# A macaron block on one core: norm of the third stage dealt over attention phases 1 and 2, maxima to their rows in two transfers

## The chip, the cores and the metric

The kernel runs on one core of one Trainium2 chip, as one program with one launch. The metric is the device time of the core in microseconds (us), the median of several executions.

## What is computed

A transformer block of three stages on x of shape (4, 256, 512), all in 32-bit floats: an FFN with half weight, attention, and the same FFN again. The FFN weights come as 4-bit numbers, W = scale[g] * (wq - (zq[g] + 1)), 512 to 2 x 1376 and back; attention has 32 heads of 16 columns with one shared key and value head, and is causal.

```python
x = x + 0.5 * ffn(layernorm(x))
x = x + attn(layernorm(x))
x = x + 0.5 * ffn(layernorm(x))
def ffn(x):
    inter = x @ w_gu
    gate, up = inter[..., :1376], inter[..., 1376:]
    return (silu(gate) * up) @ w_d
def attn(x):
    q, k, v = split(x @ Wqkv)
    scores = q @ k.T * 16 ** -0.5 + slope[h] * (pos_k - pos_q)
    return softmax(scores) @ v @ Wo
```

## The kernel before

The 1024 tokens are 8 tiles of 128. Every FFN stage runs in two halves of four tiles, numbered s = 0 to 3: s = 0 and 1 are the first FFN, s = 2 and 3 the third stage. Inside a half, 11 blocks j of the hidden width are taken in turn: gate and up matmuls (`gate_up`, L1395), silu on ACT (ScalarE), the product on DVE (VectorE), and `down` (L1421). Each product of full precision is three matmuls over a high and a low part of both operands. So an operand that comes out of PSUM is copied by ACT (the high part, `xt_high`, L643) and subtracted by DVE (the low part, `xt_low`, L892).

Attention goes sample by sample, in phases b = 0 to 3. Each phase has 12 units n; three units make a group o of 8 heads. In unit (b, n) TensorE computes `shifted_scores` (L1519, banks 4 and 5), ACT takes their exponentials (`exps`, L727), GpSimd masks them (L608), and TensorE multiplies by the values (`near_values` L1533 when n % 3 is 0, `far_values` L1544 when it is 1). ACT and DVE gather the sums (`even_heads` L737, `odd_heads` L1175, both when n % 3 is 2), TensorE swaps them (`swap_sums`, L1554), and DVE divides (`normalise`, L1188 and L1190). The output projection of a sample (`project_out`, L1561) runs one phase later, in the unit numbers that a list in TensorE's `between` gives, and DVE adds it to x (`attn_out`, L1196).

The softmax needs the row maximum first. In the phase before its own, a sample's plain scores are computed (`scores`, L1479 and L1487, banks 6 and 7, the units that `score_units` gives), and DVE reduces them (`maxima`, L1129) into `nm`. When all 12 are there, TensorE transposes `nm` (`max_transposes`, L1498), ACT copies the high part into `two` (`max_high`, L703), DVE makes the low part (`max_low`, L1136), and ACT issues four transfers (`max_to_rows`, L712) that put the 2 x 32 rows of `two` into four rows of `qp[b]`, the moving operand of the shifted scores. `shifted_scores(b, 0)` waits for them on the semaphore `m_in[b]`. Other transfers into `qp` (16 rows of constants, `constant_rows`, and the q rows, `q_to_rows`) are on the SP queue.

The third stage starts in the shadow of attention. Its first four tiles are those of samples 0 and 1. DVE takes `moments` (L843, L846), an inverse root by Newton steps (`rstd_seed`, `rstd_step`, from L852), and the normalised tile (`xn_tile`, L886), of which there are two buffers. TensorE transposes it (`ffn_transposes`, L1361). `xt` lies on the memory of `qp_c`, the operand of phase 2, so `xt_high(2, ...)` waits until the last shifted scores of phase 2 are done. Gate and up matmuls of half 2 fill TensorE in phase 3: `fill` does in unit n as many steps (three matmuls each) as the list in `fill_steps` says.

The order of the work on each engine is written out by hand: one loop over (b, n) on TensorE, ACT and DVE, each with a function `between` for all that isn't a unit's own work. Every engine runs its instructions in order. What sets the order around the change is where a call stands in these loops, and the tables of unit numbers.

```python
            for b in range(B):
                for n in range(NU):
...
                    between(b, n)
                    for unit in units[-1:]:
                        maxima(*unit)
```

## Time and profile before

| | us |
|---|---|
| median of 3 runs | 614.86 |
| lowest and highest | 614.31 and 631.7 |
| the profiled execution | 614.43 |
| its span, first to last instruction | 612.6 |

The profile shows one execution. Its times count from the start of the span. A row of a timeline gives start, length, engine, line, operation, output<-inputs, sizes, the count of merged instructions, and in square brackets how long the engine had been idle before and what released it. PEld is the weight load of TensorE (PE). ACTq and SPq are the issues of transfers on those engines' queues. In phase 0 to 3 the units of the profile are found by the tiles: `qp_a` is read in phases 0 and 3, `qp_b` in phase 1, `qp_c` in phase 2.

### The profile page before, as it was taken

What the parts mean: (1) busy time and instruction counts of PE and PEld (TensorE: products, weight loads), DVE (VectorE), ACT (ScalarE), POOL (GpSimd) and SP (SyncE); (2) the same over time, 40 slices, a digit from 0 to 9 for tenths busy, and PEclk for the clock granted to TensorE, in tenths of its full rate; (3) what the DMA queues carried; (4) which work ended last, traced back from release to release, by engine and by line L of the source; (5) the groups of instructions that cost most, each with busy time, mean ns of one, the idle gap of its engine ahead of it and who ended that gap; (6) DMA issues with size and microseconds to landing.
All of it is one profiled execution on the core that took longest, in us unless ns stands there. A gap on an engine that the chain in (4) does not pass through costs nothing.

```text
span 612.6 us, 7685 instructions
## 1 busy us (share of the span) xinstructions
PE 559.6 (91%) x2968; PEld 405.8 (66%) x2968; DVE 335.8 (55%) x705; ACT 160.7 (26%) x286; POOL 88.9 (15%) x113
## 2 busy tenths in 40 slices
PE   1399999999999999979799899699999999999997
PEld 1278777778788667656455344356678887888885
DVE  5888999866311355677467899855411245111112
ACT  1242332322111011134523444464111112111110
POOL 4678000000310000021211222131000000000000
PEclk9999999999999999989889999799999999999999
DMA  7489511099057291205843000000790000100001
GB/s 206 152 251 277 147 31 39 13 247 431 8 102 132 76 120 18 39 2 102 144 87 52 4 2 1 6 1 1 237 294 1 1 0 18 51 2 0 1 0 68
DMA packets 40267, 51.52 MB, mean 84 GB/s; under 512 B 10700, under 2 KB 28214, under 8 KB 39832
## 3 DMA queue, kind: packets, MB, share of 16 engines
q1 hardware_dynamic: 35392, 40.13, 26.5%
q0 software_dynamic: 2656, 10.57, 5.4%
q10 hardware_dynamic: 2184, 0.35, 0.4%
q8 instruction: 23, 0.38, 0.3%
q14 instruction: 12, 0.10, 0.0%
HBM read 35.82 MB, written 15.02 MB: 83 GB/s over the span
## 4 chain that ended last, share of the span: by engine, by line
PE 58%; DVE 9%; ACT 1%; DMA 1%; issue 1%; ACTq 0%; DVEq 0%
PE bank L1395 25%; PE bank L1421 12%; PE bank L1561 4%; PE bank L1487 3%; PE bank L1454 3%; DVE nm L1129 3%; PE bank L1479 3%; PE bank L1533 2%; PE bank L1519 2%; PE bank L1554 2%; DMA qp_b<-two 1%; PE bank L1435 1%; PE bank L1439 1%; DVE stats L843 1%; PE bank L1361 1%
## 5 line engine op out<-in xcount | busy, mean ns | idle before, releaser
L1421 PE MATMUL bank<-w_d,hs 128*128 128x512 f32 (+1 forms) x528 | 131.1, 396 | 3.3 <-DVE w_d L944 1.8
L1421 PEld LDWEIGHTS bank<-w_d,hs 128*128 128x128 f32 (+1 forms) x528 | 97.6, 188 | 27.9 <-issue 5.4
L953 DVE TENSOR_TENSOR hf<-sil,bank 128x512 f32<-128x512 f32 (+1 forms) x44 | 30.1, 684 | 151.9 <-PE bank L1395 151.7
L1395 PE MATMUL bank<-xt,w_far 128*128 128x512 f32 (+1 forms) x384 | 92.5, 394 | 0.0
L1395 PE MATMUL bank<-xt,w_mid 128*128 128x512 f32 x384 | 90.6, 391 | 0.0
L1395 PE MATMUL bank<-xt,w_near 128*128 128x512 f32 x288 | 73.3, 406 | 10.0 <-DVE w_near L922 9.4
L1395 PEld LDWEIGHTS bank<-xt,w_mid 128*128 128x128 f32 x384 | 72.0, 188 | 15.4 <-issue 0.5
L1395 PEld LDWEIGHTS bank<-xt,w_far 128*128 128x128 f32 (+1 forms) x384 | 69.3, 181 | 18.2
L1129 DVE TENSOR_REDUCE nm<-bank 128x2 f32<-128x512 f32 (+1 forms) x96 | 61.7, 685 | 31.5 <-PE bank L1487 31.0
L1395 PEld LDWEIGHTS bank<-xt,w_near 128*128 128x128 f32 x288 | 54.2, 193 | 24.5 <-issue 12.2
L674 ACT CAST hs<-hf 128x512 fp32r<-128x512 f32 (+1 forms) x44 | 27.3, 621 | 130.9 <-DVE hf L953 118.0
L664 ACT ACTIVATE sil<-bank 128x512 f32<-128x512 f32 (+1 forms) x44 | 26.3, 597 | 127.8 <-PE bank L1395 127.4
L959 DVE TENSOR_TENSOR hs<-hf,hs 128x512 fp32r<-128x512 f32 (+1 forms) x44 | 32.5, 739 | 19.4 <-ACT hs L674 19.3
L1361 PE MATMUL bank<-ident,xn 128*128 128x128 f32 x96 | 17.2, 327 | 22.3 <-DVE xn L886 21.8
L1188 DVE RECIPROCAL den<-bank 128x128 f32<-128x128 f32 x32 | 30.4, 949 | 9.6 <-PE bank L1554 9.6
L1454 PE MATMUL bank<-xa,wqkv 128*128 128x256 f32 x128 | 31.5, 397 | 0.0
L1361 PEld LDWEIGHTS bank<-ident,xn 128*128 128x128 f32 x96 | 13.1, 166 | 26.4 <-issue 21.1
L608 POOL TENSOR_SCALAR_AFFINE_SELECT pt_a<-pt_a 128x512 f32<-128x512 f32 x16 | 10.4, 648 | 135.9 <-ACT pt_a L727 135.9
L1479 PE MATMUL bank<-causal,ident_b 128*128 128x256 bf16 (+1 forms) x96 | 22.7, 319 | 7.1 <-DVE nm L1129 6.2
L1454 PEld LDWEIGHTS bank<-xa,wqkv 128*128 128x128 f32 x128 | 24.6, 197 | 6.1 <-issue 2.8
L727 ACT ACTIVATE pt_a<-bank 128x512 f32<-128x512 f32 x32 | 17.4, 596 | 37.2 <-PE bank L1519 37.2
L1561 PE MATMUL bank<-wo,at_t 128*128 128x512 f32 x48 | 25.0, 627 | 0.0
(148 smaller groups left out, 566.5 us busy)
## 6 DMA issues: line engine op xcount, KB each, us to landing
gate_up_part<-w_mid SPq DMA_DIRECT2D x1, 4096.0 KB, 15.5
q_rows<-qst SPq DMA_DIRECT2D x16, 256.0 KB, 4.8
w_mid<-gate_up_part SPq DMA_DIRECT2D x4, 1024.0 KB, 8.3
gate_up_part<-w_far SPq DMA_DIRECT2D x1, 3840.0 KB, 24.0
qp_a<-q_rows SPq DMA_DIRECT2D x24, 128.0 KB, 4.4
w_far<-gate_up_part SPq DMA_DIRECT2D x3, 1024.0 KB, 9.0
raw_d<-in_L_ffn_qweight_down SPq DMA_DIRECT2D x10, 256.0 KB, 3.5
x<-in_L_attn_hidden_states SPq DMA_DIRECT2D x8, 256.0 KB, 5.0
```

What stands on the lines that cost most here:

```text
L664: nc.scalar.activation(sil[0:jw(jt(s, p)), n % 2, :], gate_bank(s, p)[0:jw(jt(s, p)), :], ACT.Silu)\
L674: nc.scalar.copy(hs[0:jw(jt(s, p)), n % 2, 0, :], hf[0:jw(jt(s, p)), n % 2, :]).then_inc(h_hi, 1)
L953: nc.vector.tensor_tensor(hf[0:jw(jt(s, p)), n % 2, :], sil[0:jw(jt(s, p)), n % 2, :], up_bank(s, p)[0:jw(jt(s, p)), :], ALU.mult).then_in ...
L959: nc.vector.tensor_tensor(hs[0:jw(jt(s, p)), n % 2, 1, :], hf[0:jw(jt(s, p)), n % 2, :], hs[0:jw(jt(s, p)), n % 2, 0, :].bitcast(F32), ALU ...
L1129: nc.vector.tensor_reduce(nm[:, min(u, 1), 2 * h0 + s:2 * (h0 + heads) + s - 1:2], bank[6 + s][:, :].rearrange("p (h n) -> p h n", h=heads ...
L1188: st.did(nc.vector.reciprocal(den[:, cols], ps))
L1361: ins = nc.tensor.transpose(ps[:, k * P:(k + 1) * P], xn[:, n % 2, k * P:(k + 1) * P], ident[:, :])
L1395: ins = nc.tensor.matmul(ps[0:jw(j), :], w_gu(a, k, gu, j), xt[:, b, k, :], start=(k == 0 and q == 0), stop=(k == KT - 1 and q == 2))
L1421: ins = nc.tensor.matmul(acc(s, t)[:, :], hs[0:jw(j), n % 2, a, t * P:(t + 1) * P], w_d[0:jw(j), j, b, :], start=(p == 0 and q == 0), stop ...
L1454: ins = nc.tensor.matmul(q_bank(b, h)[:, m * S:(m + 1) * S], wqkv[:, k, (2 * h + m) * P:(2 * h + m + 1) * P], xa[:, k, :], start=(k == 0), ...
L1479: nc.tensor.matmul(ps[:, :, 4 * P // heads - P:], ident_b[:, :], causal[:, :].unsqueeze(1).to_broadcast([P, heads, P]), start=True, stop=F ...
L1561: ins = nc.tensor.matmul(out_bank(b, t)[:, :], normed(b)[:, k, t * P:(t + 1) * P], wo[:, k, :], start=(k == 0), stop=(k == KT - 1))
```

## The change

Five parts:

- The maxima of a sample go to their rows in two transfers of 32 rows instead of four of 16; for that `nm` keeps the heads of each half side by side. `m_in` counts to 32 instead of 64.
- For samples 2 and 3 the transposes of the maxima stand right behind `near_values` of unit 9, ACT's `max_high` ahead of the exponentials of unit 9, and the transfers for sample 2 one unit sooner. Those for sample 3 are issued on SP (`last_max_to_rows`).
- On DVE a new function `after(b, n)` runs behind a unit's maxima. Into it go `attn_out` of sample 1 (units 5 and 8 instead of 6 and 9) and the norm of the third stage: moments tile by tile in (1, 9), (2, 1), (2, 7), (2, 9), and the first two tiles' root and normalised tiles at (2, 6) and (2, 10). The projection steps of sample 1 move to match.
- The last two of the four tiles are normalised by ACT (`act_xn`), with a shift `nmr` = -mean * rstd that DVE makes.
- TensorE transposes tile 0 in (2, 10) and tile 1 in (2, 11), tiles 2 and 3 in (3, 0) as before. `fill_steps` takes its step out of unit 1 and puts one more into unit 7.

```diff
@@ -303,7 +305,7 @@
 
-            count = (0, 1, 2, 0, 2, 2, 0, 1, 2, 0, 2, 2, 2)
+            count = (0, 0, 2, 0, 2, 2, 0, 2, 2, 0, 2, 2, 2)
             return range(sum(count[:n]), sum(count[:n + 1]))
@@ -452,6 +454,15 @@
 
+            def last_max_to_rows(b):
+
+                sp.wait_ge(a_mhi, b + 1)
+                sp.wait_ge(a_mlo, b + 1)
+                sp.wait_ge(q_in[b], 16 * 14)
+                for r in range(2):
+                    sp.dma_start(qp[b][18 + r:83 + r:64, :, :].bitcast(F32), two[0:NH, r, :].bitcast(F32))\
+                        .then_inc(m_in[b], 16)
+
             constant_rows(0)
@@ -472,6 +483,7 @@
                 q_to_rows(3, h)
+            last_max_to_rows(B - 1)
             sp.wait_ge(a_st, 2 * NU * B)
@@ -642,6 +654,16 @@
 
+            def act_xn(s, t):
+
+                act.wait_ge(nmr_ok, 1)
+                act.wait_ge(tr_ok, tile_no("ffn", s, t) - 1)
+                tile = 4 * (s % 2) + t
+                dst = xn[:, t % 2, :].rearrange("p (k e r) -> p k e r", k=KT, e=2)
+                src = x[:, tile, :].rearrange("p (r k e) -> p k e r", k=KT, e=2)
+                nc.scalar.activation(dst, src, ACT.Identity, bias=nmr[:, t - 2:t - 1],
+                                     scale=rstd[:, tile:tile + 1]).then_inc(xn_ok, 1)
+
             def gu_high(j):
@@ -684,7 +706,7 @@
                 if b >= 2:
-                    act.wait_ge(m_in[b - 2], 64)
+                    act.wait_ge(m_in[b - 2], 32)
                 nc.scalar.copy(two[:, 0, :], kv_bank(b)[:, 0:S]).then_inc(a_khi, 1)
@@ -707,10 +729,9 @@
                 act.wait_ge(q_in[b], 16 * 14)
-                for s in range(2):
-                    for r in range(2):
-                        act.dma_start(qp[b][64 * s + 18 + r:64 * s + 19 + r, :, :].bitcast(F32),
-                                      two[s:NH:2, r, :].bitcast(F32)).then_inc(m_in[b], 16)
+                for r in range(2):
+                    act.dma_start(qp[b][18 + r:83 + r:64, :, :].bitcast(F32), two[0:NH, r, :].bitcast(F32))\
+                        .then_inc(m_in[b], 16)
@@ -799,14 +820,18 @@
                     k_high(b + 2)
-                if n == (8 if b == 0 else 9) and b + 1 < B:
-                    max_high(b + 1)
-                if n == (9 if b == 0 else 10) and b + 1 < B:
+                if (b, n) == (0, 8):
+                    max_high(1)
+                if (b, n) in ((0, 9), (1, 9)):
                     max_to_rows(b + 1)
-                if (b, n) in ((B - 2, NU - 1), (B - 1, 0)):
+                if (b, n) == (B - 2, NU - 1):
                     act.wait_ge(a_st, 2 * NU * (B - 1))
                     for t in range(2):
-                        xt_high(2, 2 * (b - B + 2) + t)
+                        xt_high(2, t)
+                        act_xn(2, t + 2)
+                if (b, n) == (B - 1, 0):
+                    for t in range(2, 4):
+                        xt_high(2, t)
@@ -815,6 +840,8 @@
                         even_heads(g)
+                    if n == 9 and 1 <= b < B - 1:
+                        max_high(b + 1)
                     exps(b, n)
@@ -1126,7 +1153,7 @@
                     dve.wait_ge(a_s, 2 * e + s + 1)
-                    nc.vector.tensor_reduce(nm[:, min(u, 1), 2 * h0 + s:2 * (h0 + heads) + s - 1:2],
+                    nc.vector.tensor_reduce(nm[:, min(u, 1), NS * s + h0:NS * s + h0 + heads],
                                             bank[6 + s][:, :].rearrange("p (h n) -> p h n", h=heads),
@@ -1273,34 +1300,42 @@
                         xn_tile(tile_no("attn", 3, 1), 7)
-                if (b, n) in ((1, 8), (1, 11), (2, 6), (2, 9)):
-                    attn_out(b - 1, int(n in (9, 11)))
-                if b == B - 2:
-                    if n == 1:
-                        dve.wait_ge(a_x, 2)
-                        moments(range(0, 2))
-                    if n == 2:
-                        rstd_seed(0, 0, 2)
-                    if n in (4, 5, 7):
-                        rstd_step(0, 0, 2)
-                    if n == 9:
-                        dve.wait_ge(a_x, 4)
-                        moments(range(2, 4))
-                    if n == 10:
-                        rstd_seed(0, 2, 4)
-                        for _ in range(3):
-                            rstd_step(0, 2, 4)
-                        st.wait()
-                        ffn_xn(2, 0)
-                        ffn_xn(2, 1)
-                    if n == 11:
-                        ffn_xn(2, 2)
-                        ffn_xn(2, 3)
+                if (b, n) in ((1, 8), (1, 11)):
+                    attn_out(0, int(n == 11))
                 if (b, n) in ((B - 2, NU - 1), (B - 1, 0)):
...
                     max_low(b + 1)
+
+            def after(b, n):
+
+                if (b, n) in ((2, 5), (2, 8)):
+                    attn_out(1, int(n == 8))
+                if (b, n) in ((1, 9), (2, 1), (2, 7), (2, 9)):
+                    tile = {(1, 9): 0, (2, 1): 1, (2, 7): 2, (2, 9): 3}[b, n]
+                    dve.wait_ge(a_x, tile + 1)
+                    moments(range(tile, tile + 1))
+                if b == B - 2:
+                    if n == 1:
+                        rstd_seed(0, 0, 2)
+                    if n in (2, 4):
+                        rstd_step(0, 0, 2)
+                    if n == 4:
+                        rstd_step(0, 0, 2)
+                    if n == 6:
+                        st.wait()
+                        ffn_xn(2, 0)
+                    if n == 9:
+                        rstd_seed(0, 2, 4)
+                    if n == 10:
+                        ffn_xn(2, 1)
+                        for _ in range(3):
+                            rstd_step(0, 2, 4)
+                        st.wait()
+                        nc.vector.scalar_tensor_tensor(out=nmr[:, :], in0=mv[:, 2:4, 0], scalar=-1.0,
+                                                       in1=rstd[:, 2:4], op0=ALU.mult, op1=ALU.mult)\
+                            .then_inc(nmr_ok, 1)
@@ -1317,6 +1352,7 @@
                         normalise(g - 2, 1)
+                    after(b, n)
             normalise(NO * B - 2, 0)
@@ -1504,7 +1540,7 @@
                 if n == 0:
-                    pe.wait_ge(m_in[b], 64)
+                    pe.wait_ge(m_in[b], 32)
                 if e >= 1:
@@ -1583,7 +1619,7 @@
                 if b in (1, 2):
-                    for q, step in enumerate(range(4, 12) if b == 1 else (1, 2, 4, 5, 6, 7, 8, 8)):
+                    for q, step in enumerate(range(4, 12) if b == 1 else (1, 2, 2, 4, 4, 5, 6, 7)):
                         if step == n:
@@ -1592,13 +1628,15 @@
                             project_out(b - 1, t, range(k, k + 1))
-                if (b, n) in ((B - 2, NU - 1), (B - 1, 0)):
-                    for t in range(2):
-                        ffn_transposes(2, 2 * (b - B + 2) + t)
+                if (b, n) in ((B - 2, NU - 2), (B - 2, NU - 1)):
+                    ffn_transposes(2, n - NU + 2)
+                if (b, n) == (B - 1, 0):
+                    for t in range(2, 4):
+                        ffn_transposes(2, t)
                 if b == B - 1:
                     fill(n)
-                if n == (8 if b == 0 else 9) and b + 1 < B:
-                    max_transposes(b + 1)
+                if (b, n) == (0, 8):
+                    max_transposes(1)
@@ -1680,6 +1718,8 @@
                             near_values(g - 1)
+                        if n == 9 and 1 <= b < B - 1:
+                            max_transposes(b + 1)
                     if n % 3 == 1 and g >= 1:
```

The first place is TensorE in unit 9 of phase 1. `bank_7<-ident,nm` is the transpose of the maxima, `bank<-wo,at_t` the output projection, `bank<-qp_b,kp` the shifted scores of a unit. Before:

```order
L1554 MATMUL bank<-den,swap 128x256
L1533 MATMUL bank<-pt_a,vp 32x256 x8
L1561 MATMUL bank<-wo,at_t 128x512
L1498 MATMUL bank_7<-ident,nm 32x128 x2
L1519 MATMUL bank<-qp_b,kp 128x512 x2
```

And in the changed kernel:

```order
L1590 MATMUL bank<-den,swap 128x256
L1569 MATMUL bank<-pt_a,vp 32x256 x8
L1534 MATMUL bank_7<-ident,nm 32x128 x2
L1597 MATMUL bank<-wo,at_t 128x512
L1555 MATMUL bank<-qp_b,kp 128x512 x2
```

The transposes moved ahead of one step of the projection; on ACT the copy that reads them moved from behind the two exponentials of that unit to ahead of them.

The second place is TensorE from unit 10 of phase 2 to unit 1 or 2 of phase 3. `bank<-qp_c,kp` are the shifted scores of phase 2, `bank<-qp_a,kp` those of phase 3, `bank<-ident,xn` the transposes of normalised tiles (four to a tile). Before:

```order
L1519 MATMUL bank<-qp_c,kp 128x512 x2
L1544 MATMUL bank<-pt_far,vp 32x128 x8
L1519 MATMUL bank<-qp_c,kp 128x512 x2
L1361 MATMUL bank<-ident,xn 128x128 x8
L1519 MATMUL bank<-qp_a,kp 128x512 x2
L1554 MATMUL bank<-den,swap 128x256
L1533 MATMUL bank<-pt_b,vp 32x256 x8
L1361 MATMUL bank<-ident,xn 128x128 x8
L1519 MATMUL bank<-qp_a,kp 128x512 x2
L1544 MATMUL bank<-pt_far,vp 32x128 x8
L1395 MATMUL bank_7<-xt,w_near 128x512 x3
```

And in the changed kernel:

```order
L1555 MATMUL bank<-qp_c,kp 128x512 x2
L1580 MATMUL bank<-pt_far,vp 32x128 x8
L1397 MATMUL bank<-ident,xn 128x128 x4
L1555 MATMUL bank<-qp_c,kp 128x512 x2
L1397 MATMUL bank<-ident,xn 128x128 x4
L1555 MATMUL bank<-qp_a,kp 128x512 x2
L1590 MATMUL bank<-den,swap 128x256
L1569 MATMUL bank<-pt_b,vp 32x256 x8
L1397 MATMUL bank<-ident,xn 128x128 x8
L1555 MATMUL bank<-qp_a,kp 128x512 x2
L1580 MATMUL bank<-pt_far,vp 32x128 x8
L1555 MATMUL bank<-qp_a,kp 128x512 x2
```

The transposes of tile 0 moved one unit up, and the first three gate matmuls are gone from unit 1 of phase 3.

The third place is DVE at the same handover, from the last Newton step of the inverse root on. `num` and `den` are the odd heads of unit 11, `xt` the low parts. Before:

```order
L869 SCALAR_TENSOR_TENSOR rstd<-nwt,rstd 128x2
L886 TENSOR_SCALAR xn<-x,mv,rstd 128x512 x2
L1175 SCALAR_TENSOR_TENSOR num<-bank,pmask,num 128x256
L1175 SCALAR_TENSOR_TENSOR den<-bank,pmask,den 128x256
L886 TENSOR_SCALAR xn<-x,mv,rstd 128x512 x2
L892 TENSOR_TENSOR xt<-bank,xt 128x4x128 x2
L1188 RECIPROCAL den<-bank 128x128
```

And in the changed kernel:

```order
L896 SCALAR_TENSOR_TENSOR rstd<-nwt,rstd 128x2
L1336 SCALAR_TENSOR_TENSOR nmr<-mv,rstd 128x2
L1202 SCALAR_TENSOR_TENSOR num<-bank,pmask,num 128x256
L1202 SCALAR_TENSOR_TENSOR den<-bank,pmask,den 128x256
L919 TENSOR_TENSOR xt<-bank,xt 128x4x128 x2
L1215 RECIPROCAL den<-bank 128x128
```

Four normalised tiles left this place: tile 0 went to unit 6, tile 1 ahead of the Newton steps, tiles 2 and 3 to ACT, and the shift came in.

## Rows read from the trace of the kernel before

**Rows 1.** The page's chain that ended last: its shares by engine.

```profile
PE 58%; DVE 9%; ACT 1%; DMA 1%; issue 1%; ACTq 0%; DVEq 0%
```

**Rows 2.** Chain in order of time, end of phase 0: start us, us, what.

```profile
294.96 0.48 ACTq L712
...
296.11 7.03 DMA qp_b<-two
```

**Rows 3.** Issues of the maxima's transfers: count, size, median us to landing. First 294.7:295.2, then 340:400.

```profile
qp_b<-two ACTq DMA_DIRECT2D x2, 16.0 KB, 6.3
...
qp_a<-two ACTq DMA_DIRECT2D x4, 16.0 KB, 2.2
```

**Rows 4.** Stretches: us, TensorE busy (count), granted clock (1 is full), DMA share, GB/s.

```profile
300.00:302.00 2.00, 0.00 (x0) 0.81 1.74 239
311.50:312.00 0.50, 0.50 (x3) 1.00 1.15 135
386.50:387.00 0.50, 0.00 (x0) 0.59 0.06 18
```

**Rows 5.** Timeline of TensorE, units 0 and 2 of phase 1.

```profile
303.18 0.80 PE L1519 MATMUL bank<-qp_b,kp 64*128 64x512 f32 x2 [4.41 <-DMA qp_b<-two]
...
308.94 3.24 PE L1454 MATMUL bank<-xa,wqkv 128*128 128x256 f32 x8
...
315.21 1.99 PE L1454 MATMUL bank<-xa,wqkv 128*128 128x256 f32 x8
```

**Rows 6.** Timelines of TensorE and ACT, units 9 and 10 of phase 1.

```profile
342.52 1.12 PE L1561 MATMUL bank<-wo,at_t 128*128 128x512 f32 x2
343.49 0.38 PE L1498 MATMUL bank<-ident,nm 128*32 128x128 f32 x2
343.80 0.50 PE L1519 MATMUL bank<-qp_b,kp 64*128 64x512 f32 x2
...
341.06 1.08 ACT L727 ACTIVATE pt_b<-bank 128x512 f32<-128x512 f32 x2 [0.68 <-PE bank L1519]
343.90 0.36 ACT L703 CAST two<-bank 32x256 fp32r<-32x256 f32 x1 [1.76 <-PE bank L1498]
```

**Rows 7.** Timeline of TensorE, end of phase 2 and phase 3.

```profile
388.00 1.09 PE L1361 MATMUL bank<-ident,xn 128*128 128x128 f32 x4 [5.10 <-DVE xn L886]
...
390.38 0.79 PE L1519 MATMUL bank<-qp_a,kp 64*128 64x512 f32 x2
391.10 1.22 PE L1554 MATMUL bank<-den,swap 128*128 128x256 f32 x2
...
394.82 0.50 PE L1519 MATMUL bank<-qp_a,kp 64*128 64x512 f32 x2
...
399.60 0.51 PE L1519 MATMUL bank<-qp_a,kp 64*128 64x512 f32 x2
...
409.33 0.96 PE L1395 MATMUL bank<-xt,w_near 128*128 128x512 f32 x3
```

**Rows 8.** Timelines of DVE and, one row, of POOL (GpSimd), end of phase 2.

```profile
378.58 1.29 DVE L1129 TENSOR_REDUCE nm<-bank 128x2 f32<-128x512 f32 x2 [0.45 <-PE bank L1487]
...
380.98 0.68 DVE L1196 TENSOR_TENSOR x<-x,bank 128x512 f32<-128x512 f32 x1
...
383.18 0.38 DVE L1136 TENSOR_TENSOR two<-bank,two 32x256 fp32r<-32x256 f32 x1
...
384.66 0.16 DVE L852 TENSOR_SCALAR nwt<-mv 128x2 f32<-128x2 f32 x1
...
387.11 2.17 DVE L886 TENSOR_SCALAR xn<-x,mv,rstd 128x512 f32<-128x512 f32 x2
389.20 0.47 DVE L1175 SCALAR_TENSOR_TENSOR num<-bank,pmask,num 128x256 f32<-128x256 f32 x1
...
389.99 1.39 DVE L886 TENSOR_SCALAR xn<-x,mv,rstd 128x512 f32<-128x512 f32 x2
...
387.52 1.29 POOL L608 TENSOR_SCALAR_AFFINE_SELECT pt_far<-pt_far 128x1024 f32<-128x1024 f32 x1 [4.48 <-ACT pt_far L727]
```

2 lines of the change are left out of this document (added).

## The prediction

> **What bounds the kernel now.** I read the chain that ended last first. The reader is to see that most of it is TensorE [rows 1]: 58% of the chain, with DVE (VectorE) at 9%. The first and the last stage are matmuls back to back, and an edit there would show at full price. The change touches the attention stage between them, so I read that stage stall by stage in the timelines of TensorE, DVE and ACT (ScalarE). I write (b, n) for unit n of phase b, as the code does. Two long stalls stand there.
>
> The first is at the start of phase 1. ACT issues four transfers that bring the maxima of sample 1 to their rows; the fourth is issued at 296.11 and takes 7.03 us [rows 2], and TensorE waits 4.41 us for it, until 303.18 [rows 5]. The same transfers take 2.2 us in a phase where nothing else is in flight [rows 3]. The difference is the company: the SP queue moves the q rows of sample 2 and then the constant rows of sample 3 at that time.
>
> The second is at the end of phase 2. TensorE waits 5.10 us, until 388.00, for the first normalised tile of stage 3 [rows 7]. DVE makes it in a row [rows 8]: x update at 380.98, then moments of two tiles, the low part of the maxima at 383.18, half a normalise, the inverse root from 384.66, two tiles at 387.11, and only at 389.20 the odd heads. Phase 3 then opens at 390.38, and its second unit stands at 394.82 [rows 7].
>
> Each stall also takes TensorE's clock from 2.4 to 1.2 GHz. It fell between 300 and 302, TensorE being idle since 298.8 (303.18 less 4.41), and was back at 311.5; in the other stall it fell between 386.5 and 387.0, idle since 382.9 [rows 4, 7]. What that costs is seen in one group of eight matmuls: 3.24 us at the low level, 1.99 at the high one [rows 5].
>
> **The change part by part.**
>
> **A, two transfers for four.** Before the start of phase 1 the order of the work stays; only the transfers become two of 32 rows each. The chain shows the second issue at 294.96 and the fourth 1.15 later [rows 2]. The median of the first two is 6.3 us to landing and the fourth took 7.03 [rows 2, 3], so I put the second at 6.6: it landed at about 301.5, the fourth at 303.14. If a transfer twice as large lands like the small one, phase 1 starts 1.7 us sooner. The lower end of the gain is 0 (the bytes are the same, and they land with the last of the four); the upper end is the whole stall, 4.4 (with the 2.2 us of the quiet phase they would be there at 297.2). I take 1.7, the row of the very transfer. The clock falls all the same, since it fell within 300 to 302 and TensorE now idles until 301.5. If it comes back sooner, up to 1.2 us more is won in the eight matmuls at 308.94 (3.24 less 1.99); the sum takes nothing of it. For sample 0, in the first FFN stage, TensorE shows no wait for these transfers: 0.
>
> A rule of the Trainium skill makes A smaller ("DMA: Bandwidth & Descriptors", section "Issuing engines are not separate DMA queues"): all queues run on the same 16 engines, and how a transfer is issued saves only the sequencer's time. The trace agrees on the sharing (7.03 us against 2.2). By the rule two saved issues count, 1.15 us, and the sum would be 0.55 less of a gain.
>
> **B, maxima sooner in phase 1.** In unit (1, 9) the transposes of the maxima move ahead of one output projection (342.52 to 343.49), and ACT's copy moves ahead of the unit's two exponentials [rows 6]. The exponentials now wait behind transposes that stand behind the values' matmuls. The transposes start at 342.52, the copy 0.41 later (343.90 less 343.49) and takes 0.36; 0.1 later two exponentials, 1.08 together [rows 6], run to 344.5. TensorE's shifted scores of (1, 10), which wait for them, stood at 343.80 and now stand at about 344.55: a loss of 0.75. The other end is 0.3, were the projection to cover more of it. The gain is nothing, since no wait for sample 2's transfers shows at the start of phase 2. DVE's moments of tile 0 go behind the second half of that unit's normalise, where DVE then waits for scores anyway: 0.
>
> **C, phase 2 and the opening of phase 3.** DVE works nearly without a gap in phase 2, so what is put ahead of the last maximum of sample 3 (378.58, done 379.87 [rows 8]) delays it. Ahead of it stand as before the moments of two tiles, one x update and one inverse root; new is one normalised tile, 0.69 (half of 1.39; half of 2.17 for a pair beside a GpSimd select [rows 8]). Besides, the two Newton steps in (2, 4) and the x update in (2, 5) now stand ahead of odd heads for which TensorE's swap matmul waits. Together 0.7 to 2.5; I take 1.8 by laying these pieces behind one another, so the maximum ends at 381.7. From there, with lengths from rows 8: x update 0.7, half a normalise 1.2, low maxima 0.3, the other half 1.2, moments of one tile 0.75, inverse root 2.45 (384.66 to 387.11), one tile 0.7, the shift 0.2, odd heads 0.8 (389.20 to 389.99). That is 8.3 us, so the odd heads end at about 390.0, as before; but before, two more tiles stood behind them. TensorE meanwhile: transposes of the maxima at 382.1, ACT's copy to 382.9, exponentials to 384.1, units 10 and 11 and the first two tiles' transposes until 388.1, and the first unit of phase 3 at 388.1 (before: 390.38). Then it waits for the odd heads until 390.1. Before, the swap stood at 391.10: 1.0 us is won there. At the high clock swap, values and the last two transposes take 3.0 us, and the second unit stands at 393.1 for 394.82: 1.7 won. ACT's two tiles (0.6 each by the length of an exponential, 1.1 at most as on DVE) end by 391.5, before TensorE wants the second. Before, the fourth unit (399.60) waited for the even heads behind DVE's two low copies and a normalise; these come 1.9 sooner, and the gate step of unit 1 is out of the way. That step comes back in unit 7, 0.96 [rows 7], of which 0.7 is not hidden. So C is -1.9 + 0.7 = -1.2 at the high clock. If the clock falls in the three gaps (382.5 to 384.1, 386.2 to 387.5, 388.6 to 390.1), 1.3 of it is lost and C is +0.1. None of these gaps is over 1.6 us, and both stalls that took the clock were of 4.4 and 5.1, so I take -1.2. The maxima's transfers, issued at 384.0 on SP, land by 387.0, and phase 3 wants them at 388.1; on SP only waits for the end of attention are queued behind them.
>
> The Trainium skill speaks against one piece of C ("SBUF — State Buffer", section "Who interferes with whom"): a VectorE operation of this kind and a GpSimd operation exclude each other, and the second waits for the whole of the first. The trace agrees: the pair at 387.11, beside the select at 387.52, took 2.17 us, the next pair 1.39 [rows 8]. By it the tile in (2, 10) costs 0.4 more, and the sum would be 0.4 less of a gain.
>
> **The sum.** -1.7 + 0.75 - 1.2 = -2.15 us against the profiled execution's 614.43 (span 612.6 and 1.8 around it): 612.3. The median of the runs shown, 614.86, is 0.4 higher, so I forecast 612.7. The new layout of the maxima (a reduce writes them side by side instead of in every second place) I cost at 0: the reduce's length is set by the 512 columns that it reads.
>
> **The rivals.**
> First, the transfers land when SP's traffic lets them, not sooner for being two. For it: each next one took longer, up to 7.03 us. Then A is 0 to -0.3, and the time 614.86 - 0.2 + 0.75 - 1.2 = 614.2. Against it: the later ones were issued into the constant rows' traffic, which two issues forestall.
> Second, the clock does better: it is back before or within the matmuls from 303 to 311.5. At half clock at most 4.1 of these 8.3 us are lost; 2.8 of them won back gives 609.9. Against it: the stall is still 2.7 us long.
> Third, slower than before: DVE's queue in phase 2 becomes the bound of the handover. Place: the odd heads of (2, 11), now behind the inverse root, a tile and the shift. Price: the maximum 2.5 late instead of 1.8, the tile beside a select 0.4, the clock fallen across the opening of phase 3 1.3, and still low for units 1 to 3 with their gate step (4 us of matmuls at twice the time, half of it hidden) 2.0: 4.4 on 612.7 is 617.1. It decides from C = +0.95 on, that is when the odd heads end after about 391 with the clock low.
> Fourth, the change does not do what it says, for nothing waited for the maxima of samples 2 and 3, so that sooner brings nothing: this is so by the trace and is in the forecast already.
>
> **How the numbers follow.** Forecast 0.50 (611.5 to 613.9), first rival 0.17, second 0.20, third 0.13. The range reaches to 609.5 for the second and to 616.5 for the third, which leaves its far end out. A measurement of this kernel can tell about 2%, 12 us, from no change, and no case comes near: faster 0.01, within 0.98, slower 0.01.
>
> **What would show it.** Right: phase 1 starts near 301.5; a new stall of 0.7 us before unit (1, 10); the 5.10 us stall gone, and in its place three of 1 to 2 us (before unit (2, 10), before the transposes of (2, 11), before the first swap of phase 3). Wrong: the second transfer for sample 1 takes 8 us; the last maximum of phase 2 is not later than before (then DVE was no bound there); the clock is at 1.2 GHz while phase 3 opens; an ACT table load stands beside the new tiles.

## The result and the profile after

| | before | changed |
|---|---|---|
| median, us | 623.04 (4 runs) | 623.21 (4 runs) |
| lowest and highest | 614.31 and 631.7 | 620.6 and 624.42 |
| the profiled execution | 614.43 | 624.42 |
| its span | 612.6 | 622.7 |

The ratio of comparable runs is 1.0135, 95% interval 1.0071 to 1.0199. (Two executions of before, at 631 us, are disturbed and not in the ratio; they are why the two medians look equal.) Forecast were 612.7 us, 0.35% less than before, and a range up to 616.5. The change makes the kernel slower.

The chain that ended last has the shares of before [rows 1], with one point more for DMA:

```profile
PE 58%; DVE 9%; DMA 2%; ACT 1%; issue 1%; SPq 0%; DVEq 0%; ACTq 0%
```

For the rest I measure stages by one kind of mark: the start of each unit's shifted scores in TensorE's timeline (every length below is the difference of two such starts; where no clock or transfer comes in they repeat within 0.02 us from run to run). Over the attention stage, in us:

| from, to | before | changed | difference |
|---|---|---|---|
| (0, 0) to (0, 11) | 38.52 | 43.15 | +4.63 |
| (0, 11) to (1, 0) | 4.91 | 5.16 | +0.25 |
| (1, 0) to (1, 9) | 37.40 | 37.65 | +0.25 |
| (1, 9) to (1, 10) | 3.22 | 3.78 | +0.56 |
| (1, 10) to (2, 0) | 8.17 | 8.16 | 0 |
| (2, 0) to (2, 9) | 26.41 | 30.91 | +4.50 |
| (2, 9) to (3, 0) | 12.00 | 9.24 | -2.76 |
| (3, 0) to (3, 3) | 9.22 | 12.20 | +2.98 |
| (3, 3) to (3, 11) | 17.30 | 17.98 | +0.68 |

The sum, +11.1, is the difference of the spans (10.1) and the 1.1 us by which (0, 0) started sooner. The rows answer to steps A (second and third), B (fourth) and C (the last four, +5.4). The first row is +4.2 in unit (0, 2) and +0.5 in (0, 3), and nothing elsewhere. TensorE, ACT and DVE have the same instructions there; only the columns of `nm` that DVE writes are others. I take it as not the change's, and the first two experiments bear on that.

TensorE's timeline of the changed kernel, the marks and the waits:

```profile
306.99 0.80 PE L1555 MATMUL bank<-qp_b,kp 64*128 64x512 f32 x2 [4.66 <-DMA qp_b<-two]
```

```profile
348.42 0.50 PE L1555 MATMUL bank<-qp_b,kp 64*128 64x512 f32 x2 [0.56 <-ACT pt_b L748]
...
366.63 0.70 PE L1590 MATMUL bank<-den,swap 128*128 128x256 f32 x2 [1.31 <-DVE den L1202]
...
376.88 1.22 PE L1590 MATMUL bank<-den,swap 128*128 128x256 f32 x2 [1.57 <-DVE den L1202]
...
386.68 0.39 PE L1515 MATMUL bank<-causal,ident_b 128*128 128x256 bf16 x2 [1.64 <-DVE nm L1156]
...
392.76 0.50 PE L1555 MATMUL bank<-qp_c,kp 64*128 64x512 f32 x2 [1.42 <-ACT pt_b L748]
...
396.14 0.66 PE L1397 MATMUL bank<-ident,xn 128*128 128x128 f32 x4 [1.15 <-DVE xn L913]
...
399.56 1.22 PE L1590 MATMUL bank<-den,swap 128*128 128x256 f32 x2 [2.33 <-DVE den L1202]
...
404.38 0.50 PE L1555 MATMUL bank<-qp_a,kp 64*128 64x512 f32 x2
```

Row by row: the wait for the maxima of sample 1 is as long as before (4.66 for 4.41 [rows 5]). A new wait of 0.56 stands before unit (1, 10). The swap matmul waits 1.31 and 1.57 us for `den`, in units (2, 3) and (2, 6): before, it waited for nothing there, as the row of unit (2, 6) below shows. The 5.10 us wait [rows 7] is gone, and 1.64, 1.42, 1.15 and 2.33 have come for it. The second unit of phase 3 stands 7.65 us behind the first, for 4.44 before [rows 7].

```profile
369.39 0.70 PE L1554 MATMUL bank<-den,swap 128*128 128x256 f32 x2
```

DVE (VectorE) in the same units, `nwt` and `rstd` being the inverse root, `num` and `den` the odd heads:

```profile
364.47 0.85 DVE L879 TENSOR_SCALAR nwt<-mv 128x2 f32<-128x2 f32 x1
...
365.70 0.48 DVE L1202 SCALAR_TENSOR_TENSOR num<-bank,pmask,num 128x256 f32<-128x256 f32 x1
...
374.50 0.95 DVE L896 SCALAR_TENSOR_TENSOR rstd<-nwt,rstd 128x2 f32<-128x2 f32 x1
...
375.96 0.48 DVE L1202 SCALAR_TENSOR_TENSOR num<-bank,pmask,num 128x256 f32<-128x256 f32 x1
```

```profile
382.27 1.29 DVE L1156 TENSOR_REDUCE nm<-bank 128x4 f32<-128x512 f32 x2 [2.46 <-PE bank L1523]
...
388.11 1.28 DVE L1156 TENSOR_REDUCE nm<-bank 128x2 f32<-128x512 f32 x2
...
396.39 0.96 DVE L896 SCALAR_TENSOR_TENSOR rstd<-nwt,rstd 128x2 f32<-128x2 f32 x1
...
398.63 0.48 DVE L1202 SCALAR_TENSOR_TENSOR num<-bank,pmask,num 128x256 f32<-128x256 f32 x1
399.03 0.48 DVE L1202 SCALAR_TENSOR_TENSOR den<-bank,pmask,den 128x256 f32<-128x256 f32 x1
```

And GpSimd's selects (POOL), of which two stand here:

```profile
374.36 1.09 POOL L620 TENSOR_SCALAR_AFFINE_SELECT pt_far<-pt_far 128x1024 f32<-128x1024 f32 x1 [2.73 <-ACT pt_far L748]
...
396.24 1.09 POOL L620 TENSOR_SCALAR_AFFINE_SELECT pt_far<-pt_far 128x1024 f32<-128x1024 f32 x1 [1.09 <-ACT pt_far L748]
```

Two things are to be seen. The odd heads come right behind pieces of the inverse root (the seed before 365.70, two steps before 375.96), and TensorE waits for them. And an operation on two elements a partition, 0.16 us alone, takes 0.95 when it meets a select: the one at 374.50 ends at 375.45, and the select that began at 374.36 ends at 375.45 too; the one at 396.39 ends at 397.35, the select at 397.33.

The granted clock, in stretches of the timeline (columns as in rows 4):

```profile
272.00:276.00 4.00, 4.00 (x26) 0.50 0.00 2
...
305.50:315.00 9.50, 7.75 (x35) 0.50 0.54 116
366.60:376.50 9.90, 8.59 (x68) 1.00 0.00 0
377.00:380.50 3.50, 3.50 (x19) 0.53 0.02 5
...
387.50:390.50 3.00, 2.87 (x18) 0.50 0.00 0
...
398.00:404.00 6.00, 4.44 (x25) 0.50 0.01 3
```

Five stretches at 1.2 GHz, 37.5 us together (264.3 to 277.9, 305.2 to 315.5, 376.9 to 380.3, 387.1 to 390.6, 397.4 to 404.2); before had three, 20.5 us together (263.7 to 267.1, 301.3 to 311.5, 386.6 to 393.4). The first two lie behind the same waits in both. That it stayed low for 13.7 us instead of 3.4 in phase 0 goes with the +4.6 of the table: 10.2 us more at half the clock are at most 5.1 us.

### The profile page after: what moved, and what is told of

Same layout as the page of the kernel before. It is cut to its first block, busy times and chain, and to the rows that moved or that the text cites. A ratio compares the mean times of both kernels' runs of the same rounds, so it can differ in the third digit from the quotient of the medians.

```text
span 622.7 us, 7679 instructions
## 1 busy us (share of the span) xinstructions
PE 567.5 (91%) x2968; PEld 410.3 (66%) x2968; DVE 336.2 (54%) x704; ACT 162.8 (26%) x288; POOL 89.2 (14%) x113
## 4 chain that ended last, share of the span: by engine, by line
PE 58%; DVE 9%; DMA 2%; ACT 1%; issue 1%; SPq 0%; DVEq 0%; ACTq 0%
PE bank L1431 25%; PE bank L1457 11%; PE bank L1597 3%; PE bank L1523 3%; PE bank L1569 3%; PE bank L1490 3%; DVE nm L1156 3%; PE bank L1515 2%; PE bank L1590 2%; DMA qp_c<-q_rows 2%; PE bank L1555 1%; PE bank L1471 1%; PE bank L1475 1%; PE bank L1580 1%; DVE xn L913 1%
```

## The experiments

Two theories stood at first. G: the added waits take the clock, so the loss stays whatever is done about the maxima. L: the loss is luck, the clock behind a wait that the change doesn't touch. All ratios are to before on the same chip, by comparable runs, with the 95% interval.

**e1, the changed kernel again.** No edit.

> The changed kernel as it is, timed against the kernel before in 5 rounds, to see how far each of them varies from run to run. Theory G (the gaps: the change puts work on DVE ahead of odd heads and of maxima, TensorE gets gaps of 1.3 to 2.3 us in phase 2 and at the opening of phase 3, and its clock falls in them): the profile again shows three falls of the clock between 370 and 405 us, and TensorE waits before the swaps; time 620 to 625. Theory L (luck: the time lost is the clock that happened to stay low after the stall at 262 us, which the change doesn't touch): this run varies as the kernel before does (614 to 632), and in a run where the clock comes back by 268 us the changed kernel is at 616 to 621.

Measured: 618.16 us, 1.0066 [1.0042, 1.0091]. In its profiled execution:

```profile
266.00:272.00 6.00, 5.78 (x21) 0.50 0.00 0
272.50:280.00 7.50, 6.74 (x58) 1.00 0.00 1
```

So both hold in part. The median lies below G's 620, but its three falls of the clock are there, and both waits for `den`. The clock in phase 0 came back at 272.5, not 277.9, and (0, 0) to (0, 11) took 40.56 us instead of 43.15: that share of the first result was luck. The rows of B and C repeat: (1, 9) to (1, 10) 3.77, (2, 0) to (2, 9) 30.80, (2, 0) to (3, 11) 70.48 for 70.33. Those of A do not: (0, 11) to (1, 0) is 4.25 for 5.16, (1, 0) to (1, 9) 36.77 for 37.65. What the change itself costs is 0.7%, 4 us.

**e2, two transfers alone.** The kernel before, with

```diff
-                for s in range(2):
-                    for r in range(2):
...
+                for r in range(2):
+                    act.dma_start(qp[b][18 + r:83 + r:64, :, :].bitcast(F32), two[0:NH, r, :].bitcast(F32))\
+                        .then_inc(m_in[b], 16)
```

and the layout of `nm` and the counts of `m_in` that go with it.

> The kernel before with nothing but two transfers of 32 rows instead of four of 16, for all samples. If transfers are bound by their issue (my step A) phase 1 starts 1.7 us sooner and the time is 1 to 3 us less. If the traffic of SP's queue binds them (the first rival) the stall at the end of phase 0 stays within 0.3 us of 4.41 and the time is the kernel's before, within 0.5 us, each state of the clock taken for itself.

Measured: 614.22 us, 1.0008 [0.998, 1.0037]. Nothing is gained. Its chain has the second transfer at

```profile
295.22 8.68 DMA qp_b<-two
```

that is, 0.55 us behind ACT's first issue, where the fourth of before stood 1.83 behind it (294.28 and 296.11): 1.3 us sooner, and 1.65 longer (7.03 [rows 2]). The interval leaves at most 1.2 us of gain, less than the 1.7 of step A.

**e3, the changed kernel with the maxima at their old place.** Phases 1 and 2:

```diff
-                if (b, n) == (0, 8):
-                    max_high(1)
...
+                if n == (8 if b == 0 else 9) and b + 1 < B:
+                    max_high(b + 1)
...
-                    if n == 9 and 1 <= b < B - 1:
-                        max_high(b + 1)
                     exps(b, n)
```

the same for `max_transposes`, and the transfers of sample 2 issued in unit 10.

> The changed kernel with the transposes and the high part of the maxima back in their old places (behind the exponentials of unit 9), transfers for sample 2 back in unit 10. Step B says that the gap of 0.56 us before unit (1, 10) and that of 1.42 us before unit (2, 10) go: 0.6 to 0.8 us less from phase 1, and up to 1 us less from phase 2, where DVE is late anyway. Theory G: it stays slower than the kernel before by 3 us or more, since the gaps on DVE's account stay. Theory L: no difference beyond the luck of the clock.

Measured: 618.5 us, 1.0067 [1.0039, 1.0095], that of e1. (1, 9) to (1, 10) is back at 3.22, but (2, 0) to (3, 11) is 70.52. The loss is not in the maxima. Its chain and TensorE's timeline hold one surprise:

```profile
296.35 5.52 DMA qp_b<-two
```

```profile
301.92 0.50 PE L1553 MATMUL bank<-qp_b,kp 64*128 64x512 f32 x2 [1.62 <-DMA qp_b<-two]
```

With the same two transfers the second took 5.52 us here, 7.63 in e1, 8.68 in e2, and (0, 11) to (1, 0) is 2.13 us for 4.91 before: this one time phase 1 did start sooner. Its company was the same (SP's six issues of q rows begin 2.1 us ahead of ACT's first issue here, 2.0 in e1, 1.9 in e2), so why it landed sooner is open. And though TensorE waited only 1.62 us, the clock was at 1.2 GHz from 302.6 to 309.4.

**e4, the maxima sooner alone.** The kernel before with the edit that e3 undoes, four transfers on ACT kept.

> The kernel before with only the transposes and the high part of the maxima ahead of the exponentials of unit 9 in phases 1 and 2, and the transfers for sample 2 one unit sooner; four transfers. Step B says 0.6 to 0.8 us slower in phase 1 (unit 10 waits for the exponentials). In phase 2 TensorE's unit 10 waits as well, 1 to 1.5 us, which the wait of 5.10 us for the first normalised tile swallows. Time 0.5 to 1 us above the kernel before in the same state of the clock.

Measured: 616.14 us, 1.0028 [1.0004, 1.0052]. (1, 9) to (1, 10) is 3.77, as in the changed kernel: this is B's price. The next unit takes 3.34 for 2.99, but that belongs to this run alone: with two transfers it is 2.98 in the changed kernel and 2.99 in e1. Sample 3's earlier maxima bring nothing back: (2, 0) to (3, 11) is 65.86, where e2 has 65.95.

So the loss of C should lie in where the norm stands. By units, (2, 3) to (2, 4) lost 1.4 us, its wait of 1.31, and (2, 6) to (2, 7) 3.2, its wait of 1.57 and 1.6 more with the clock low; both stand right behind the pieces put ahead of odd heads. The other units up to (2, 7) differ by projection steps that were moved, and even out within 0.2 us.

**e5, the norm behind the odd heads.** The changed kernel, with

```diff
-                if (b, n) in ((1, 9), (2, 1), (2, 7), (2, 9)):
-                    tile = {(1, 9): 0, (2, 1): 1, (2, 7): 2, (2, 9): 3}[b, n]
+                if (b, n) in ((1, 9), (2, 2), (2, 7), (2, 9)):
+                    tile = {(1, 9): 0, (2, 2): 1, (2, 7): 2, (2, 9): 3}[b, n]
...
-                    if n == 1:
+                    if n == 2:
                         rstd_seed(0, 0, 2)
-                    if n in (2, 4):
+                    if n in (3, 5):
                         rstd_step(0, 0, 2)
-                    if n == 4:
+                    if n == 5:
                         rstd_step(0, 0, 2)
```

> The changed kernel, with the norm work that stood ahead of odd heads in phase 2 put behind them: moments of tile 1 and the seed from unit 1 to 2, one Newton step from unit 2 to 3, two from unit 4 to 5. Same work, same count of instructions. Theory P (place): phase 2 lost 4.4 us between (2, 0) and (2, 9) because these pieces delay odd heads, TensorE's swap waits 1.31 and 1.57 us for them, and the second wait takes the clock. Then (2, 0) to (2, 9) falls from 30.9 us to 27 to 28.5, both waits for den go or fall under 0.5, and the kernel is 2 to 4 us faster than the changed one. Rival W (work): DVE is full in phase 2 and it is the added normalised tile and what it has to do, not its place, that sets the end; then (2, 0) to (2, 9) stays over 30 and the time within 1 us of the changed kernel.

Measured: 615.73 us, 1.0032 [1.0001, 1.0062]. (2, 0) to (2, 9) is 26.96 for 30.91, within 0.6 of before: theory P. TensorE's and DVE's timelines:

```profile
368.76 0.70 PE L1590 MATMUL bank<-den,swap 128*128 128x256 f32 x2
...
377.20 0.39 PE L1515 MATMUL bank<-causal,ident_b 128*128 128x256 bf16 x2 [1.85 <-DVE nm L1156]
...
389.97 0.70 PE L1590 MATMUL bank<-den,swap 128*128 128x256 f32 x2 [2.32 <-DVE den L1202]
```

```profile
378.64 1.27 DVE L1156 TENSOR_REDUCE nm<-bank 128x2 f32<-128x512 f32 x2
```

The swap at 368.76, which waited 1.57 us, waits for nothing, and (2, 3) to (2, 4) takes 2.99 us as before. The last maximum of phase 2 starts 27.5 us behind (2, 0); in the changed kernel it was 31.5, before 26.6. So the norm's work delays it by 0.9 us, and its place did by four more. The clock, which fell right behind the 1.57 us wait in the changed kernel, in e1 and in e3, stayed at 2.4 GHz until 377.5. Left is the opening of phase 3, with its wait of 2.32.

**e6, ACT's tiles alone.** The kernel before, where tiles 2 and 3 leave DVE:

```diff
                         ffn_xn(2, 0)
                         ffn_xn(2, 1)
-                    if n == 11:
-                        ffn_xn(2, 2)
-                        ffn_xn(2, 3)
+                        nc.vector.scalar_tensor_tensor(out=nmr[:, :], ...)
```

and `act_xn(2, t + 2)` behind `xt_high(2, t)` on ACT, as in the change.

> The kernel before with one part of the change alone: tiles 2 and 3 are normalised by ACT from a shift that DVE makes behind tiles 0 and 1; nothing else moves. If ACT's tiles are what opens phase 3 badly (they took 1.33 us each in the changed kernel, ahead of the exponentials of unit (3, 0)), (3, 0) to (3, 3) grows from 9.2 us by 1 to 2 here and the kernel is 0.5 to 1.5 us slower than before. If the bad opening comes from the order on DVE (inverse root and tile 1 ahead of the odd heads), (3, 0) to (3, 3) stays within 0.7 of 9.2 here and the time within 0.5 us of before, or up to 1 less, since DVE is rid of 1.39 us.

Measured: 616.36 us, 1.0023 [0.9987, 1.0058]: too close to call. (3, 0) to (3, 3) is 10.10, but with before's order there it is anything from 9.2 to 10.2 in the profiles of e2, e4, e7 and e8 as well. ACT's timeline, though, is plain:

```profile
387.49 1.33 ACT L654 ACTIVATE xn<-x,nmr,rstd 128x512 f32<-128x512 f32 x1
...
389.19 1.33 ACT L654 ACTIVATE xn<-x,nmr,rstd 128x512 f32<-128x512 f32 x1
390.41 1.08 ACT L739 ACTIVATE pt_a<-bank 128x512 f32<-128x512 f32 x2
```

A tile costs ACT 1.33 us, twice my 0.6, and the exponentials of (3, 0) stand behind both.

**e7, the q rows held.** The kernel before. SP waits before the second half of sample 2's q rows, and so before the constant rows behind them (the loop over the halves is written out for that):

```diff
-            for h in range(2):
-                q_to_dram(2, h)
-                q_to_rows(2, h)
+            q_to_dram(2, 0)
+            q_to_rows(2, 0)
+            q_to_dram(2, 1)
+            sp.wait_ge(m_in[1], 64)
+            q_to_rows(2, 1)
```

> The kernel before, but SP issues the second half of sample 2's q rows (six transfers of 128 KB), and the constant rows behind them, only when the maxima of sample 1 have landed. Theory S (the maxima land with SP's traffic, whatever their number): the fourth transfer takes 2 to 3.5 us instead of 7.03, TensorE's wait before unit (1, 0) falls from 4.4 to under 1 us; the scores of sample 2, which need the held rows, then wait 3 to 6 us in unit (1, 0), so the kernel is within 2 us of before, on either side. Rival F (a fixed cost of these 16-row writes): the fourth still takes over 5 us with nothing beside it, and the kernel is 4 us or more slower.

Measured: 616.85 us, 1.0046 [1.0014, 1.0078]. Its chain, and TensorE's timeline:

```profile
295.09 2.88 DMA qp_b<-two
...
300.22 5.96 DMA qp_c<-q_rows
```

```profile
299.07 0.50 PE L1521 MATMUL bank<-qp_b,kp 64*128 64x512 f32 x2 [1.32 <-ACT pt_far L729]
306.23 1.04 PE L1481 MATMUL bank<-causal,ident_b 128*128 128x512 bf16 x2 [6.66 <-DMA qp_c<-q_rows]
```

The fourth transfer takes 2.88 us, like the quiet 2.2 of [rows 3]: theory S. What is left of the wait, 1.32, is for exponentials. (0, 11) to (1, 0) is 1.82 us for 4.91, so A could hardly have won more than 3.1 us, and the transfers' number was not what it hung on. The held rows are then late themselves (6.66), and the kernel as a whole is slower.

**e8, a projection in the wait.** The kernel before. The eight matmuls that cost 3.24 us behind the wait [rows 5] go ahead of it:

```diff
-                if (b, n) in ((0, 8), (0, 10), (1, 0), (1, 2)):
+                if (b, n) in ((0, 8), (0, 10), (1, 2)):
...
+                    if (b, n) == (1, 0):
+                        project_q(3, 1, range(4))
                     shifted_scores(b, n)
```

> The kernel before, with the eight matmuls halves of the q projection of sample 3 that stand in unit (1, 0) put ahead of its shifted scores, into the wait for the maxima. If the wait's price is TensorE's idle time and the clock that it takes, the wait falls from 4.4 to about 2.4 us, the eight matmuls no longer cost 3.24 us behind it, and the kernel is 2 to 4 us faster than before. If the q work was hidden behind the maxima of sample 2 on DVE (4.29 us idle there, waiting for TensorE), the gain is under 1 us.

Measured: 609.92 us, 0.9934 [0.9894, 0.9973], faster than both kernels.

```profile
300.18 1.99 PE L1454 MATMUL bank<-xa,wqkv 128*128 128x256 f32 x8
304.66 0.50 PE L1519 MATMUL bank<-qp_b,kp 64*128 64x512 f32 x2 [2.49 <-DMA qp_b<-two]
```

The wait is 2.49 and (1, 0) to (1, 1) takes 6.55 us for 9.49, 2.9 less. By the ratio the kernel gained 4.1 us (1.7 to 6.5). The profiled execution is one of the slower of the eleven, at 613.78: four lie from 613.6 to 615.6 and seven from 607.0 to 611.0. What the seven have over it no profile shows.

**e9, odd heads first.** The kernel of e5, with the opening of phase 3 loosened. On DVE, in unit 11, and on ACT:

```diff
                         ffn_xn(2, 1)
-                        for _ in range(3):
-                            rstd_step(0, 2, 4)
+                        rstd_step(0, 2, 4)
...
+                if (b, n) == (B - 2, NU - 1):
+                    for _ in range(2):
+                        rstd_step(0, 2, 4)
...
-                        act_xn(2, t + 2)
+                if (b, n) == (B - 1, 0):
+                    act_xn(2, 2)
+                    act_xn(2, 3)
```

The shift stands behind the two steps; transposes and copies of tile 3 go to (3, 1).

> The kernel of e5 with the opening of phase 3 loosened: on DVE the odd heads of unit (2, 11) stand ahead of two of the three Newton steps and of the shift; on ACT the exponentials of (3, 0) stand ahead of its two tiles; the transposes and copies of tile 3 go to unit (3, 1). Theory O (the rest of C's loss is the odd heads behind the inverse root and the exponentials behind ACT's tiles): in e5 the swap of (3, 0) stood at 2.8 us behind that unit's scores, with TensorE waiting 2.32 us for den; that wait falls under 1 us and (3, 0) to (3, 3) falls from 11.5 us to 9 to 10, so the kernel is 1.5 to 2.5 us faster than e5, at a ratio of about 1.000 to before. Rival T (the tiles themselves are late): TensorE waits for ACT's tile 2 instead, by 1.5 us or more, and (3, 0) to (3, 3) stays over 11.

Measured: 614.43 us, 0.9992 [0.9962, 1.0022]. (3, 0) to (3, 3) is 10.28, (2, 0) to (3, 11) 64.19: below before's 64.93 for the first time in a kernel with the change's order. TensorE, and its clock:

```profile
388.41 0.70 PE L1594 MATMUL bank<-den,swap 128*128 128x256 f32 x2 [0.95 <-DVE den L1203]
...
391.48 0.63 PE L1401 MATMUL bank<-ident,xn 128*128 128x128 f32 x4 [1.37 <-ACT xn L664]
```

```profile
377.50:380.50 3.00, 3.00 (x17) 0.50 0.00 0
382.00:395.00 13.00, 7.68 (x76) 1.00 0.02 6
```

The wait for `den` fell from 2.32 to 0.95 (theory O), one of 1.37 for ACT's tile came (a part of T), and the clock does not fall there in this execution. That is not sure to be the order's doing: in e11, with the same opening, it fell at 387.3 and (3, 0) to (3, 3) took 11.08 us.

**e10, the whole projection.** As e8 with all sixteen matmuls: `project_q(3, 1)`.

> As e8, with all sixteen matmuls of the q projection of sample 3's second half ahead of the first shifted scores of phase 1 (from units 0 and 2). In e8 the wait left over was 2.49 us and the clock still fell. If idle time is what takes the clock, the wait is now about 0.5 us, the clock stays at 2.4 GHz from (1, 0) on, and (1, 0) to (1, 1), 6.55 us in e8, falls to 5 or less: 2 to 4 us faster than e8, 6 to 9 faster than before. If the clock falls all the same, or the q rows of sample 2 bind next, it is within 1.5 us of e8.

Measured: 612.6 us, 0.9974 [0.9944, 1.0003]: a miss. The profiled execution, 608.92, did what was foreseen:

```profile
297.36 3.72 PE L1454 MATMUL bank<-xa,wqkv 128*128 128x256 f32 x16
301.54 0.50 PE L1519 MATMUL bank<-qp_b,kp 64*128 64x512 f32 x2 [0.47 <-DMA qp_b<-two]
...
309.40 0.60 PE L1479 MATMUL bank<-causal,ident_b 128*128 128x512 bf16 x2 [1.33 <-DVE nm L1129]
```

A wait of 0.47, the clock up, (1, 0) to (1, 1) 3.86 us. But with unit 2 emptied, TensorE waits 1.33 for a maximum of sample 2, and there the clock fell (310.1 to 313.5). Over (1, 0) to (1, 9) it is 32.96 against 34.51 in e8, and still the ratio is 0.004 behind e8's, though the two intervals overlap. Why most executions gained less than the profiled one is open.

**e11, all mends together**: the changed kernel with the edits of e5, e9 and e8, and sample 2's maxima at their old place. **e12, e8 again** beside it.

> The changed kernel with all mends: norm behind odd heads (e5), opening of phase 3 as in e9, the eight matmuls in the wait (e8), and sample 2's maxima back behind the exponentials of (1, 9). If the parts add up: e9 stood at 0.999 of before, e8 at 0.993, and unit (1, 10) gives 0.56 us back, so 0.991 to 0.993, about 609.5 us where before is 614.6; (1, 9) to (1, 10) is 3.2 again, (2, 0) to (3, 11) 64.2. If the clock's answer to a removed stall eats the gain, as it may have in e10, 0.996 or more.

> The kernel of e8 again, beside e11 on one chip. It stood at 609.92 us, 0.9934, its profiled execution at 613.78 with TensorE's clock low from 264.2 to 271.5 and again to 312.0. If the spread of 607 to 615 is how long the clock stays low behind the waits, a profiled execution near 608 has these stretches 3 to 4 us shorter each, and the lengths of all other units unchanged within 0.1; median 608 to 611.

Measured for e11: 614.4 us where before has 615.54, 0.9946 [0.9913, 0.9979]. (1, 9) to (1, 10) is 3.22, (2, 0) to (3, 11) 64.32, as foreseen; the ratio is 0.002 worse than the product of e8's and e9's, within its interval. Its twelve executions spread from 608.87 to 628.84 us. It beats before and the changed kernel, but not e8, by anything that these runs can tell. e12 gave no ratio: its six executions lie between 605.61 and 628.05 us, too far apart for one. Its profiled execution, 611.35, has (1, 0) to (1, 1) at 5.39 us instead of e8's 6.55, as foreseen, with the clock back at 306.1 instead of 312. The expectation that the rest stays the same was wrong. TensorE in e12, its clock, and the same place in before:

```profile
342.40 0.39 PE L1479 MATMUL bank<-causal,ident_b 128*128 128x256 bf16 x2 [1.17 <-DVE nm L1129]
...
345.31 0.60 PE L1479 MATMUL bank<-causal,ident_b 128*128 128x256 bf16 x2 [0.48 <-DVE nm L1129]
```

```profile
344.00:350.00 6.00, 5.52 (x27) 0.50 0.02 4
```

```profile
348.40 0.39 PE L1479 MATMUL bank<-causal,ident_b 128*128 128x256 bf16 x2 [1.17 <-DVE nm L1129]
...
351.31 0.39 PE L1479 MATMUL bank<-causal,ident_b 128*128 128x256 bf16 x2 [1.03 <-DVE nm L1129]
```

```profile
311.50:380.00 68.50, 63.15 (x511) 1.00 0.13 25
```

The wait of 1.17 us and the next left the clock alone in before, and in e8, the same kernel as e12. In e12 it fell at 343.6, 1.2 us behind the first of them and ahead of the second, at 2.3 us' cost ((1, 11) to (2, 1) 10.45 for 8.18).

## Why the prediction was wrong

**The reading of the bound** was right as far as it went: the two long stalls were the places to look at, and e8 shows that some 4 us can be had at the first.

**A failed.** The forecast was -1.7 from "if a transfer twice as large lands like the small one". It does not: beside SP's traffic the second of two took 5.52 to 8.68 us (five profiles, their mean 7.6) and the fourth of four 6.74 to 7.07 (six). So what is issued 1.3 us sooner mostly lands no sooner: (0, 11) to (1, 0) is 4.25 to 5.28 us in the profiles with two transfers, the 2.13 of e3 apart, and 4.62 to 4.95 in those with four, and e2 stands at 1.0008. The first rival (the transfers land when SP's traffic lets them) was the better account: e7 shows that the traffic sets the time, and e3's 5.52 that it does not set it alone. The sentence from the Trainium skill that I cited against A ("DMA: Bandwidth & Descriptors", "Issuing engines are not separate DMA queues") agrees with that; even its 1.15 us for two saved issues were not seen, the exception of e3 apart.

**B held**, +0.56 for +0.75: the wait for ACT's exponentials is where it was put.

**C failed, and it decides the sign.** Forecast -1.2, measured +5.4 in the profile (+5.55 in e1). Taken apart:

The failing step is the line "Together 0.7 to 2.5; I take 1.8 by laying these pieces behind one another", for the delay of the last maximum of sample 3. It came 4.9 us later. Laying pieces behind one another on DVE counts their lengths, and e5 shows that their lengths are worth 0.9. The other four came from a loop that the sum did not have: a piece ahead of odd heads delays TensorE's swap; the scores stand behind the swap in TensorE's queue, so DVE itself then waits (2.46 us of idle time on DVE before the maximum at 382.27), and the clock fell behind the wait of 1.57. I had named the two steps in (2, 4) as standing ahead of odd heads, and priced them at their length. I had misread two places: the moments of tile 1 and the seed in (2, 1) stand ahead of odd heads too, and the wait of 1.31 came behind them, while the x update in (2, 5) stands behind them (377.94 against 375.96).

The chain on DVE from that maximum to the end of the odd heads was put at 8.3 us and took 10.1 (389.39 to 399.51). In it are two meetings with selects that the sum did not have (0.56 at 394.61 and 0.96 at 396.39, 1.2 us more than the lengths alone) and a wait of 0.59 for ACT.

"The clock holds in the gaps" was the second failing step. "None of these gaps is over 1.6 us, and both stalls that took the clock were of 4.4 and 5.1, so I take" the high clock: the clock fell behind 1.57, behind 1.64, and behind 1.15 at the start of the 2.33. Two examples of a fall at long waits say nothing about short ones. The prediction had the clock at 1.2 GHz in the opening of phase 3 among its signs of being wrong, and priced such falls at 1.3 us.

Third, ACT's two tiles were taken from the length of an exponential, 0.6 each, and measured 1.33, more than the bound of 1.1. With them ahead of the exponentials of (3, 0), these started 5.0 us behind their scores (401.69 against 396.73), for 0.9 before. In e6, with both tiles ahead of them but the rest as before, it is 2.2. The rest is not the tiles' length: 1.37 us of it is idle time on ACT, which waited for the shift from DVE. The tile's strided input and output may be why it takes 1.33; no run here separates that. e9 undid this and the order on DVE together, and gained 1.3 us in (2, 0) to (3, 11); the share of each stays open.

Right in C: the 5.10 us wait went (-2.76 in that row, and it is the gain that was meant), and the fill step cost 0.68 for my 0.7.

**The Trainium skill's sharing rule** ("SBUF — State Buffer", "Who interferes with whom") was weighed for one tile at 0.4 us. The trace agrees, and shows it for the shortest operations too: one of the thirteen small operations of an inverse root ran 0.8 us longer beside a select, at 374.50.

**The third rival** (DVE's queue becomes the bound of the handover, the clock falls) was the right kind, at 617.1; e1's median is 618.16. Its place was wrong in part: most of the loss sat earlier, in the waits of (2, 3) and (2, 6). At 13% it had too small a chance, and the range was cut short of it.

Open stays how much of each kernel's spread (before: 611.1 to 619.9 us over 33 executions beside e5 to e8) is the clock behind waits in phase 0. (0, 2) to (0, 3), the same instructions in all kernels, took 4.95 to 9.26 us in the profiles. The two longest, 9.26, are both of kernels with the new layout of the maxima (the changed one and e11); five others with it took 4.96 to 7.13 and seven without it 4.95 to 7.35, and e2 stands at 1.0008, so I take it for luck, but fourteen profiles don't settle it. Nor is the clock all of the spread: (0, 0) itself starts anywhere from 256.55 (e4) to 261.38 us (e3), with the granted clock at 2.4 GHz until then in every profile.

## What to carry to other kernels

Work that is moved for better balance is priced by what is queued behind it on its engine, and by who waits for that, not by its length: put filler behind the operation that another engine waits for. Before shortening a transfer, look at what shares the queues with it: here holding the other traffic took it from 7.03 to 2.88 us (and made that traffic late), and halving the count did nothing that the runs can tell. A wait that can't be removed is a place for independent matmuls, and the small edit that used it won 4.1 us by the ratio of e8, about what the whole change lost.

## What the runs showed of the hardware

The clock's answer to a wait is not fixed. Behind the same 1.69 us wait in phase 0 it stayed at 1.2 GHz for 3.4 us in before, 6.8 in e1 and 13.7 in the changed kernel. Behind a wait of 1.17 us it fell in e12 and not in e8, which is the same kernel; behind one of 1.85 in unit (2, 8) it fell in e5, and behind 1.86 in the same place of e11 it did not. The one unit (0, 2) differs by 4.3 us between profiles for that reason, so stages must be compared by their lengths, not spans.

A VectorE operation of 0.16 us that meets a GpSimd select ends with the select, within 0.03 us: 0.54 to 0.96 us in seven places of the kernels before and changed.

ACT took 1.33 us for a tile of 128 x 512 between two SBUF buffers with a scale and a bias, against 0.54 for an exponential of that size out of PSUM.
